# A macaron block on one core: another order of loads at the front, scatters in four parts, and new places for the work beside the expert slots

## The reference

```python
x = x + 0.5 * ffn(layernorm(x))
x = x + attn(layernorm(x))
x = x + 0.5 * ffn(layernorm(x))

# ffn: one of 8 experts per token (argmax of a softmax router)
gates = max(softmax(xt @ Wr + br)); idx = argmax(...)
h = relu(xn @ W1[idx] + b1[idx])          # 256 -> 1024
y = (h @ W2[idx] + b2[idx]) * gates       # 1024 -> 256
# attn: down 256 -> 64, three gated layers, each with a causal convolution
# of 4 taps, two 64x64 gates, a scan over time (h = a*h_prev + g) and an
# rms norm; then up 64 -> 256
```

## Time and profile before

| | us |
|---|---|
| median of 3 runs | 768.86 |
| the profiled execution | 763.67 |
| its span | 761.9 |
| PE busy in the span | 684.7 (90%) |
| DVE, ACT, POOL busy | 410.7, 264.3, 172.7 |
| start of the first norm of a slot | 59.33 |
| start of the first product of slot 0 | 62.04 |

### The profile page before, as it was taken

The page is one execution under the profiler, slowest core; times in us unless marked ns, Lnnn a source line. Parts: engine busy times, 40 slices in busy tenths (PEclk is TensorE's granted clock), DMA queues, the critical chain, the costliest instruction groups (busy, mean ns, idle before and its releaser), DMA issues.

```text
span 761.9 us, 15311 instructions
## 1 busy us (share of the span) xinstructions
PE 684.7 (90%) x4350; PEld 594.2 (78%) x4350; DVE 410.7 (54%) x1427; ACT 264.3 (35%) x630; POOL 172.7 (23%) x178
## 2 busy tenths in 40 slices
PE   5548889899999999998997798989999889999993
PEld 4437679899988877887775686878888789999992
DVE  6466356333346576856877585865667332333331
ACT  3123112322334557343644454432522223222230
POOL 4622551111121120251212511240124111111111
PEclk9557899999999999999996898998999999999997
DMA  8989453665564444255253305353536464454440
GB/s 259 279 289 379 154 195 105 234 201 203 180 218 138 158 164 138 78 184 199 73 177 105 113 15 208 126 183 110 180 99 220 155 199 148 139 197 133 159 136 13
DMA packets 59919, 126.51 MB, mean 166 GB/s; under 512 B 8105, under 2 KB 36660, under 8 KB 59700
## 3 DMA queue, kind: packets, MB, share of 16 engines
q1 hardware_dynamic: 53204, 108.50, 43.7%
q0 software_dynamic: 6624, 16.92, 6.0%
HBM read 106.36 MB, written 20.35 MB: 166 GB/s over the span
## 4 chain that ended last, share of the span: by engine, by line
PE 80%; issue 6%; DVE 6%; ACT 2%; another core or an unknown queue 2%; DVEq 2%; DMA 1%; POOL 0%; SPq 0%; ACTq 0%; POOLq 0%
PE bank L1631 33%; PE bank L1645 33%; PE bank L1546 2%; PE bank L1618 2%; PE bank L1486 2%; PE bank L1551 1%; DVE st L717 1%; PE bank L1556 1%; PE bank L1538 1%; PE bank L1566 1%; PE bank L1577 1%; PE bank L1501 1%; PE bank L1514 1%; DMA rows<-in_L_attn_h 1%
## 5 line engine op out<-in xcount | busy, mean ns | idle before, releaser
L1645 PE MATMUL bank<-w,act_t 128*128 x1184 | 287.0, 393 | 9.3 <-issue 7.7
L1631 PE MATMUL bank<-mn_t,w 128*128 128x128 f32 x2368 | 287.3, 278 | 3.9 <-issue 3.9
L1631 PEld LDWEIGHTS bank<-mn_t,w 128*128 128x128 f32 x2368 | 278.7, 195 | 10.5 <-issue 10.2
L1645 PEld LDWEIGHTS bank<-w,act_t 128*128 128x128 f32 x1184 | 225.6, 197 | 48.9 <-issue 20.0
L1136 DVE TENSOR_SCALAR act_t<-bank,vec 128x128 f32<-128x128 f32 x296 | 83.5, 344 | 122.2 <-PE bank L1631 101.0
L1367 ACT ACTIVATE mn_t<-bank,vec 128x128 f32<-128x128 f32 x152 | 61.4, 454 | 230.3 <-PE bank L1618 215.2
L1377 ACT ACTIVATE act_t<-bank,vec 128x128 f32<-128x128 f32 x296 | 85.0, 368 | 105.8 <-PE bank L1631 76.5
L1143 DVE TENSOR_TENSOR y_b<-bank,b_all 128x256 f32<-128x256 f32 x74 | 31.4, 424 | 119.9 <-PE bank L1645 105.2
L625 POOL DMA_INDIRECT out_x<-res,pay x37 | 36.4, 984 | 243.4 <-DVE res L1149 242.8
L625 POOL DMA_INDIRECT x_middle<-res,pay x37 | 39.7, 1074 | 216.9 <-DVE res L1149 215.5
L616 POOL DMA_INDIRECT routed_rows<-rows,dest x64 | 63.5, 992 | 51.9 <-DVE dest L817 34.5
(11 more groups left out here) (211 smaller groups left out, 456.6 us busy)
## 6 DMA issues: line engine op xcount, KB each, us to landing
w<-in_L_ffn_W SPq DMA_DIRECT2D x82, 1024.0 KB
pay<-routed_rows SPq DMA_DIRECT2D x78, 130.0 KB, 2.1
rows<-in_L_attn_h SPq DMA_DIRECT2D x8, 512.0 KB, 6.9
rows<-x_middle SPq DMA_DIRECT2D x8, 512.0 KB, 5.1
routed_rows<-fill SPq DMA_DIRECT2D x2, 1040.0 KB, 10.7
b_all<-in_L_ffn_b SPq DMA_DIRECT2D x1, 1024.0 KB
routed_rows<-rows,dest POOLq DMA_INDIRECT x64
x_middle<-res,pay POOLq DMA_INDIRECT x37, 3.2
```

The lines of the kernel that those rows point to most:

```text
L1631: last = t.matmul(b_hid[half][:, c % 4 * P:(c % 4 + 1) * P], w1[i % W1S][:, k * F + c * P:k * F + (c + 1) * P], mn_t[p][i % 2][:, k * P:(k ...
L1645: last = t.matmul(b_out[i % 2], act_t[i % 2][:, c * P:(c + 1) * P], w2[:, ds(eb * (WE // FC) + c * D, D)], start=c == 0, stop=c == FC - 1)
```

## The change

Five things change. (1) SP issues input chunk 0 first, then the router weights, chunk 1, the router bias (with a semaphore of its own), the second weights of four experts (4 MB), chunks 2 and 3, and then the parameters. Behind the tables, one more expert's second weights go ahead of the first slots' rows, and the fill goes last; so the scatters no longer wait for the fill, and the rows of every stage but the first do. (2) On ACT and PE the exponentials of chunks 0 and 1 and the ranks of chunk 0 stand half a chunk earlier. (3) `route` takes a quarter of a chunk (two scatters) rather than half of one (four), and each quarter has a place of its own. (4) On DVE `centre_down` stands ahead of the last part of the tables, and the moments of chunk 3 go from ahead of the first slot to places 0 and 1. (5) Nearly all other places in the tables at the top are new.

```diff
@@ places (five of them; nearly all others change as well)
-R_CHOOSE = [[None, None, 1, 120], [1417, 1872, 2304, 2736]]
+R_CHOOSE = [[None, None, 1, 96], [1441, 1968, 2424, 2904]]
-CONVOLVE = [[1032, 1296, 1705, 2112], [1153, 1464, 1829, 2280], [1277, 1632, 2042, 2472]]
+CONVOLVE = [[1033, 1321, 1708, 2209], [1154, 1536, 1969, 2401], [1296, 1706, 2256, 2736]]
-R_SCATTER = [[[None, None], [None, None], [24, 25], [96, 97]], [[744, 745], [1008, 1009], [1176, 1177], [1392,
-    1393]]]
-TABLE_PARTS = [[[None, None, None, None, None, None], [217, 240, 264, 336, 337, None]], [[1514, 1609, 1658, 1659,
-    1660, 1704], [2041, 2064, 2066, 2067, 2137, 2138], [2400, 2425, 2473, 2474, 2475, 2520], [2809, 2832, 2833,
-    2834, 2835, None]]]
+R_SCATTER = [[[None, None, None, None], [None, None, None, None], [25, 48, 49, 72], [73, 74, 96, 97]], [[744, 745,
+    746, 768], [1008, 1009, 1032, 1033], [1224, 1225, 1226, 1248], [1464, 1488, 1489, 1490]]]
+TABLE_PARTS = [[[None, None, None, None, None, None], [169, 192, 240, 264, 265, None]], [[1513, 1560, 1561, 1562,
+    1563, 1608], [2066, 2088, 2089, 2090, 2091, 2136], [2473, 2496, 2497, 2498, 2499, 2544], [2977, 3000, 3001,
+    3002, 3003, None]]]
@@ next_rows (SP)
                     s = FIRST[p].index(i)
+                    if (p, s) != (0, 0):
+                        sp.wait_ge(s_fill[p], 16)
                     sp.wait_ge(s_tab, tables_at(p, s))
@@ the front of SP
+            load_x(0, 0)
             sp.dma_start(wr[:, :].rearrange("p (k e) -> p k e", k=KD),
                          router_w.rearrange("(k p) e -> p k e", p=P)).then_inc(s_rt, 16)
-            sp.dma_start(rb_all[:, :], router_b[None, :].to_broadcast([P, E])).then_inc(s_rt, 16)
-            load_x(0, 0)
             load_x(0, 1)
-            sp.wait_ge(s_c2, 1)
-            empty_rows(0)
+            sp.dma_start(rb_all[:, :], router_b[None, :].to_broadcast([P, E])).then_inc(s_rb, 16)
+            for e in range(EAGER):
+                second_weights(e)
             load_x(0, 2)
-            second_weights(0)
+            load_x(0, 3)
             load_parameters()
-            load_x(0, 3)
-            for e in range(1, EAGER):
-                second_weights(e)
+
             sp.wait_ge(s_tab, 1)
             slot_weights(0, 0)
+            sp.wait_ge(s_order, 1)
+            second_weights_by_use(0)
             for i in range(RING - 1):
                 next_rows(0, i)
-            sp.wait_ge(s_order, 1)
             for i in range(1, W1S):
-                second_weights_by_use(i - 1)
                 slot_weights(0, i)
-            for k in range(W1S - 1, LATER):
+                second_weights_by_use(i)
+            for k in range(W1S, LATER):
                 second_weights_by_use(k)
+            empty_rows(0)
@@ route (POOL)
-            def route(f, c, b):
+            def route(f, c, part):
                 pool.wait_ge(s_ds[f], c + 1)
-                pool.wait_ge(s_fill[f], 16)
-                for j in range(TPC):
-                    t = (b * NC + c) * TPC + j
+                for k in range(2 * part, 2 * part + 2):
+                    t = (k // TPC * NC + c) * TPC + k % TPC
@@ the front of DVE
+            centre_down()
             tables(0, 0, 5)
-            centre_down()
-            for c in range(HC, NC):
-                for b in range(NB):
-                    moments(R1, c, b)
+            for b in range(NB):
+                moments(R1, 2, b)
@@ the front of ACT
-            for part in range(2):
-                keep(R1, 1, part)
+            keep(R1, 1, 0)
             exponentials(0, 0)
+            keep(R1, 1, 1)
@@ the front of PE
-            for part in range(2):
-                transposes(R1, 1, part)
+            transposes(R1, 1, 0)
+            ranks(0, 0)
+            transposes(R1, 1, 1)
             logits(R1, 1)
-            ranks(0, 0)
```

102 lines of the change are left out of this document (53 added, 49 removed).

## The result

The changed kernel took 761.7 us (median of 15 runs, 756.01 to 765.06), the kernel before 768.27 us beside it (15 runs, 765.09 to 772.32, and one of 1760.94 that stays unexplained and does not move the median). The ratio is 0.9906 with a 95% interval of 0.9884 to 0.9928: 0.7 to 1.2% faster, 7 us where 22 were forecast. The profiled execution took 758.34 us against 763.67.

What follows compares the result with a forecast made beforehand. PE, busy 90% of the span, was taken as the bound, leaving its gaps, its clock and the front. Terms -5.1 - 4 - 7 - 4 - 4 + 2 = -22.1 us gave 741.6 profiled, 746.8 us median; range 731 to 767.

Steps and rivals of the forecast that it cites:

- Slot 21 of pass 1: Its tables and last scatters come later, so SP blocks at place 60: +2 us, ends 0 and +6.
- the other places: Remaining moved places keep every instruction and most gaps to PE's next step: 0 us, from -4 to +4.
- the start of pass 1: Convolution and `choose` go behind the first norms, so the norm comes sooner: -4 us, ends -6.1 and 0.
- slot 4: In pass 1, tables one slot sooner free SP's queue and the weights behind: -4 us, ends -4.3 and 0.
- The front: Up to the first norm: earlier chunk 0 work, and chunk 3's moments moved behind the first slots: -5.1 us.
- my cover of about 1 us: In front, rows of slots 0 to 3 land near 53 us, while DVE is busy until 54.2.
- Pass 0's scatters: Runs of chunks 2 and 3 split into two, four, six and four: -4 us, ends -12.9 and +7.4.
- The 12.9 us: PE time that the two scatter runs of chunks 2 and 3 in pass 0 cost before the change.
- The four chunks of the second feed-forward: Runs of eight scatters become 6+2, 4+4, 6+2 and 2+6: -7 us, ends -14.4 and +5.
- The first one: POOL's density, not run length, decides, so both scatter terms (-11 us) vanish: 758 to 766 us, chance 0.17.
- The second rival: The stall grows with POOL's queue, from near the sixth indirect DMA, stores counted: 783 us, chance 0.09.
- The signs: Profile after: first norm near 54 us, PE's turns under 12 us apart at scatters, ACT's unnamed idle under 8 us.

Runs made afterwards that it cites:

- e9: The kernel before, unedited, run again in a set without stalls: 731.14 us.
- e8: The changed kernel, unedited, run again in a set without stalls: 732.84 us, ratio 1.0041 to the kernel before.
- e4: The changed kernel with `ranks` of chunk 0 back behind `logits` of chunk 1 on PE: 762.69 us, ratio 0.9871 to the kernel before.
- e13: The changed kernel with the 1.04 MB fill issued early, behind chunk 3's load: 726.09 us, ratio 0.9938 to the kernel before, without stalls.
- e17: The changed kernel with the fill issued later, behind slot 5's rows: 753.01 us, ratio 0.986 to the kernel before, with stalls.
- e18: The changed front with old places, second feed-forward's scatters spread with pauses, fill behind slot 5's rows: 745.76 us, ratio 0.9751 to the kernel before, with stalls.
- e15: The changed front with old places, second feed-forward's scatters spread with pauses, fill issued early: ratio 0.9948 to the kernel before, without stalls.
- e3: The changed kernel with all split runs of scatters cut four and four, one place apart: 758.37 us, ratio 0.9832 to the kernel before.

## Why the prediction was wrong

**The step that failed** is the one that priced the moved places. "Slot 21 of pass 1: +2" and "the other places keep every instruction ... so I take 0" stood against -4 for the start of pass 1 and -4 for slot 4. The two gains were measured at -5.1 and -4.3 us, and slots 13 to 21 at +11.6, 72.31 against 60.72 us, in the profiles without stalls. Of the 4.3 us at slot 4 all is PE work that left the stretch (5.7 us less there; PE's idle time there was 3.3 us in e9 and 3.6 in e8), and of the 5.1 us 2.4 are. I counted a stretch as won when an instruction left it, and asked of the place where it arrives only whether somebody waits there. PE is busy 90% of the span; what leaves one stretch must be run in another at its full price, 8.7 us here. Only idle time that nobody fills again is a gain. In the two profiles with stalls, where 5.3 us came of 22.1, slots 13 to 21 took 14.8 us more, by far the largest part of what is missing.

**The front** (-5.1 forecast): -3.6 without stalls, -2.5 with them, and nothing of it left at slot 37. DVE's part came as worked out (moments of chunk 3 gone, 4.0 us), and so did the chain ahead of the scatters (the first at 19.81 instead of 21.34). With stalls the tables were 0.9 us later all the same. Without them they were complete at 36.73 against 38.10 in e9, and the first norm then waited 2.22 us for its rows, behind 1 MB more: my cover of about 1 us was too small (with stalls 0.82 us of waiting). I did not ask who waits behind `ranks` on PE, which stood still for 2.41 us there; e4 leaves open what that costs. Some 2 us of the -3.6 are doubtful, since chunk 0's rows were placed at 22.42 in e9's one profile and at 20.20 in the first. What I left out is the fill: the diff moves it from the head of the queue to behind the weights, ahead of slot 4's rows, and e13 and e17 put about 0.5 to 1% on this alone.

**Pass 0's scatters** (-4): +0.7 between the two profiles, of it +0.8 by stalls. The 12.9 us could not be had by the scatters alone. Without stalls the same slots take as long (79.41 against 79.97 us): DVE waits 7.88 us there for slot 4's rows behind a full DMA queue, 383 GB/s from 60 to 80 us. Two causes hid behind each other, and I took the whole sum for the one that I had found. Once the fill is out of the way, the split does count: in one set with stalls slots 0 to 9 took 75.80 us in e17, which splits these scatters, and 83.79 in e18, which has them in eights. Without stalls, with the fill early, it is 73.72 (e13) against 75.28 (e15). So about 6 us of the term lay behind the fill, an estimate from these four profiles; e18 with pass 0's scatters split was not run.

**The four chunks of the second feed-forward** (-7): -4.6 by stalls (23.4 against 18.8 us over slots 9 of pass 0 to 21 of pass 1), the sign and the kind right. It is -3.9 and -5.1 at chunks 1 and 2, +1.1 and +3.2 at chunks 0 and 3. Only four and four was a real gap on POOL, as I had it; "one slot apart" was none for the others. Chunk 2's 5.1 us are not explained by the length of its row, which is nine DMAs before and after.

**The rivals.** The first one, runs not split where it counts, gave 758 to 766 us, and 761.7 lies there. Its mechanism, that the runs are not really split, holds for three of the four chunks, though the rest of the miss is the places', which no rival had. By the rule of the Trainium skill, SBUF — State Buffer, section "Who interferes with whom", PE and ACT never wait on anyone. In sets of one kind they do stand still: ACT for 9.49 us beside e3's row of nine. In the other kind none does with the same instructions, so these alone don't bring it; what ACT waited on, a port or something else, is open. The second rival (+7.4 us in pass 0, 783 us) did not come; its count from the sixth DMA on is near what the rows show (PE's first gap beside chunk 3's row opens at 605.45, with the seventh DMA at 605.26), but only that place paid so much.

**The signs.** Against the forecast the first norm came at 56.82 and not near 54, PE's turns around chunk 2's scatters lay 13.2 us apart (72.30 to 85.49) and ACT stood still for 9.53 and 9.38 us beside the second feed-forward's. As forecast the first norm of pass 1 (407.86) followed the last product (406.21) at once, SP issued slot 4's rows at 443.17, 9 us ahead of its turn, and PE waited 2.34 and 1.55 us in front of slot 21.

**The chances.** Faster by over 1% (below 761.2) had 0.71; 761.7 is just within 1%, which had 0.19. That it came out faster at all hung on the kind of the set, which the forecast did not know: in one without stalls the same change gave 1.0041. A profile from one set was all that the forecast knew, and the largest term rested on waits whose cause it did not show.

## What to carry to other kernels

Before a term is called a gain, balance it: sum the busy engine's work in every stretch before and after, and count as won only idle time that stays away; moved work is paid where it arrives. Read a queue from its head: each load that an edit moves counts for everything behind it while the DMA engines are full, be it 1 MB of constants. And where waits have a releaser that the profile can't name, run the kernel again in another set before building on them.
